# Third stage of a fused two-layer block: raw-weight loads 0 and 1 and context loads 2 and 3 issued from ScalarE instead of SyncE

## The chip, the cores and the metric

One NeuronCore of a Trainium2 chip runs the whole program. The metric is the device time of one execution in microseconds (us). Five engines work from their own instruction queues and meet through semaphores: TensorE (PE, matmuls), VectorE (DVE), ScalarE (ACT), GpSimd (POOL) and SyncE (SP), which only waits and issues DMAs. Both SP and ACT can issue DMAs; each has a DMA queue of its own (q1 is fed by SP, q10 by ACT in the profile), and the data are moved by the core's 16 DMA engines.

## The reference, cut to what matters

The program computes four residual blocks on x of 2048 tokens by 512 features (4 batches of 512). Each normalizes x first.

```python
x = x + _L0_xattn_ref(_layernorm(x), ctx_2048)                        # stage a: fp8-rounded product with the context
x = x + _L0_ffn_ref(_layernorm(x), gate_w, up_w, down_w, gate_s, up_s, down_s)   # stage b: SiLU-gated FFN, 1408 hidden
x = x + _L1_xattn_ref(_layernorm(x), ctx_2048, mask)                  # stage c: attention over the context
x = x + _L1_ffn_ref(_layernorm(x), w_gate, w_up, w_down)              # stage d: Hadamard-rotated ternary FFN, 2048 hidden

# _L1_xattn_ref
scores = einsum('bsd,bmd->bsm', hidden_states, memory_tokens) / sqrt(D)
scores = where(mask, scores, -1e30)
readout = einsum('bsm,bmd->bsd', softmax(scores), memory_tokens)

# weights of _L1_ffn_ref
scale = clip(mean(abs(w)), EPS)
wq = clip(round(w / scale), -1, 1) * scale
```

## The kernel before

The 2048 tokens are 16 tiles of 128 rows (NT = 16); four tiles share one context (TPB = 4), so contexts 0 to 3 serve tiles 0 to 3, 4 to 7, 8 to 11 and 12 to 15. Everything lives in SBUF in one hand-divided arena. Stages a and b are interleaved tile by tile and end at about 321 us; stage c, the "third stage", follows, and stage d takes the rest. No scheduler is involved: on each engine the order is that of the code, and every dependence is a semaphore that the code names.

Stage c, for tile k, in the order in which the tile passes through the engines:

- ACT normalizes the tile (`x_normal`, L775) and takes its fp16 high part (`x_high`, L782); POOL makes the low part (`x_low`, L494).
- SP turns both parts with two transposing DMAs, `c_x_turn` (L379 for the high part, L381 for the low one). Its buffer is one of two, so it waits until the scores of tile k-2 are done.
- PE makes the scores (`scores`, L1764, 16 matmuls of 128x512). DVE adds the mask and takes the row maximum (L1369, L1372), ACT takes the exponential (L817) and its fp16 high part (`p_high`, L788), POOL the low part (`p_low`, L499).
- SP turns both parts, `c_p_turn` (L387, L389), once the readout of tile k-2 is done.
- PE makes the readout (`readout`, L1782, 16 matmuls), and DVE adds it to X (L1354).

PE's order is scores(0), scores(1), scores(2), readout(0), scores(3), readout(1), scores(4), and so on: scores(k), readout(k-2).

Two more streams run beside this. The raw contexts (1 MB transposed and 1 MB plain each, `ctx2_load`, L370) are split into fp16 high and low parts: ACT makes the high parts (`context_high_parts`, L797), POOL the low parts (L505), except those of context 0, which DVE makes (L1439, semaphore `c_cv_first`). `conversions(k)` does part k mod 4 of context k/4+1 at tile k. The readout of tile 0 needs all four low parts of context 0. And the stage-d weights come in twelve raw chunks of 1 MB (`w1_load`), in two buffers: ACT takes the sign of w + threshold (`w1_sign`, L809), DVE rounds to ternary (`round_weights`, L1211). Chunk n is signed at tile n+1 and rounded at tile n+2; chunks 0 and 1 are loaded by SP (L394), chunks 2 to 11 by ACT (L801) right behind the sign of chunk n-1. The buffer of chunk 0 overlaps the down weights of stage b, that of chunk 1 the buffers of the earlier weight sums. Stage d begins with turns of tile 0 that wait for chunk 11 of 12 to be rounded.

In SP's order the weight loads stand between `c_x_turn(1)` and `c_x_turn(2)`, behind a wait for all residual sums of stage b (`b_add`, made by DVE at L1220); context load 2 stands between `c_x_turn(3)` and `c_p_turn(1)`, and context load 3 between `c_x_turn(7)` and `c_p_turn(5)`.

Of the kernel before, what the change touches and what calls it, by code (L numbers as in the profile page):

```python
# [7 lines left out]
P = 128  # L8
NT = T // P
TPB = NT // B  # L10
# [17 lines left out]
def fused_blocks(nc, x, ctx_t, ctx_n, mask, gate_t, up_t, down_t, gate_s, up_s, down_s,  # L28
# [7 lines left out]
    with ExitStack() as ctx:  # L36
# [79 lines left out]
        w1raw = [cut(24, 2048), cut(84, 2048)]  # L116
# [103 lines left out]
        def wait(eng, s, v):  # L220

            if not isinstance(v, int) or v > 0:
                eng.wait_ge(s, v)
# [32 lines left out]
        def at(k, n):  # L256

            return isinstance(k, int) and k == n
# [19 lines left out]
        def on(j):  # L278

            return not isinstance(j, int) or 0 <= j < NT  # L280
# [6 lines left out]
        def w1_chunk(n):  # L287

            if n < 8:
                return w1_src[n // 4][:, n % 4, :]  # L290
            return w1_src[2][:, 4 * (n - 8):4 * (n - 8) + 4, :]

        @block.sync
        def _(sp):
# [67 lines left out]
            sp.wait_ge(ds_ps, 1)  # L362
            sp.wait_ge(a_add, NT)
            def ctx2_load(e):
                if e == 2:
                    sp.wait_ge(c_cv_first, TPB)
                if e == 3:
                    sp.wait_ge(c_cv_lo, TPB)
                for t, src in enumerate((ctx_t, ctx_n)):
                    sp.dma_start(ctx_raw[e % 2][:, t, :, :], src[e].rearrange("(k p) m -> p k m", p=P)).then_inc(ctx2_in[e % 2], 16)  # L370

# [16 lines left out]
                sp.wait_ge(c_pl_r, j + 1)  # L388
                sp.dma_start_transpose(c_plT[u], c_pl[u]).then_inc(c_pq[u], 16)  # L389

            def w1_load(n):
                if n >= 2:
                    sp.wait_ge(w1_done, n - 1)
                sp.dma_start(w1raw[n % 2], w1_chunk(n)).then_inc(w1_in[n % 2], 16)  # L394

            c_x_turn(0)
            sp.wait_ge(w1a_done, 3 * NT)
            c_x_turn(1)
            sp.wait_ge(b_add, NT)
            w1_load(0)  # L400
            w1_load(1)
            for k in range(NT):
                if k < NT - 2:
                    c_x_turn(k + 2)
                if k in (1, 5):
                    ctx2_load(2 + k // 5)
                c_p_turn(k)

            def y_turn(j):
# [152 lines left out]
        def _(act):  # L562
# [227 lines left out]
            def context_high_parts(e, i):  # L790
# [5 lines left out]
                    wait(act, c_ro, TPB * (e - 1))  # L796
                nc.scalar.activation(ctx_p[e % 2][0][:, t, kk:kk + 2, :], ctx_raw[e % 2][:, t, kk:kk + 2, :], ACT.Copy).then_inc(c_cv_hi, 1)  # L797

            def w1_load(n):
                act.wait_ge(w1_done, n - 1)  # L800
                nc.scalar.dma_start(w1raw[n % 2], w1_chunk(n)).then_inc(w1_in[n % 2], 16)  # L801

            def w1_sign(n):
# [7 lines left out]

            def c_body(k, u):
                if on(k):
                    act.wait_ge(c_neg, 2 * k + 2)
                    wait(act, c_pl_r, k - 1)
                    wait(act, c_norm, 2 * k - 2)
                    nc.scalar.activation(c_p[u], bank(2 + u), ACT.Exp, bias=c_sm[:, u, 1:2], scale=SM_SCALE,  # L817
                                         accum_out=c_sm[:, u, 2:3]).then_inc(c_p_r, 1)
                    p_high(k)
                    if on(k + 3):  # L820
                        x_normal(k + 3)
                    if on(k + 3):
                        x_high(k + 3)
                    for e, i in conversions(k):
                        context_high_parts(e, i)
                    if 1 <= k < 13:
                        w1_sign(k - 1)
                    if 2 <= k < 12:
                        w1_load(k)
                if at(k, NT - 2):  # L830
                    d_high(0)
                if at(k, NT - 1):
                    d_round(0, 0)
                if at(k, NT):
                    d_turned(0, 0)
                    d_high(1)
# [1161 lines left out]
```

## Time and profile before

| what | value |
|---|---|
| time, median of 3 runs (lowest to highest) | 723.27 us (718.18 to 724.7) |
| the profiled execution: time, span in the profile | 720.0 us, 718.2 us |
| busy: PE, DVE, ACT, POOL | 91%, 82%, 66%, 51% of the span |
| LDWEIGHTS (PEld) busy | 52% |
| q1 (SP): packets, MB, share of the 16 engines | 167188, 71.94 MB, 43.4% |
| q10 (ACT): the same | 3408, 11.27 MB, 4.8% |
| chain that ended last, by engine | PE 48%, DVE 22%, ACT 10%, issue 7%, POOL 6%, DMA 5% |
| stage c in the span | about 321 to 445 us |

The page shows one execution. Busy shares are averages over the four stages; a wait is read from the timeline, where the number in brackets behind a row is the idle time of the engine just before it and what ended it. "SPq" and "ACTq" rows are DMA issues: their length is the time that the issuing queue was held, not the time of the transfer. The granted clock (PEclk) is 1.00 at 2.4 GHz and 0.50 at 1.2 GHz.

### The profile page before, as it was taken

What the parts mean: (1) busy time and instruction counts of PE and PEld (TensorE: products, weight loads), DVE (VectorE), ACT (ScalarE), POOL (GpSimd) and SP (SyncE); (2) the same over time, 40 slices, a digit from 0 to 9 for tenths busy, and PEclk for the clock granted to TensorE, in tenths of its full rate; (3) what the DMA queues carried; (4) which work ended last, traced back from release to release, by engine and by line L of the source; (5) the groups of instructions that cost most, each with busy time, mean ns of one, the idle gap of its engine ahead of it and who ended that gap; (6) DMA issues with size and microseconds to landing.
All of it is one profiled execution on the core that took longest, in us unless ns stands there. A gap on an engine that the chain in (4) does not pass through costs nothing.

```text
span 718.2 us, 12556 instructions
## 1 busy us (share of the span) xinstructions
PE 653.0 (91%) x4086; PEld 375.3 (52%) x4086; DVE 589.5 (82%) x1386; ACT 472.8 (66%) x965; POOL 368.5 (51%) x291
## 2 busy tenths in 40 slices
PE   1788899999999999997999999997999999999996
PEld 0365566656666676752444444444444445444543
DVE  6889899999998888365877764788999899999874
ACT  3747467766776556375878833567787887778734
POOL 2023032323232413165767631079999998999970
PEclk9999899999999999998999999999999999999999
DMA  8971233333341322718999930445556655655611
GB/s 215 249 257 23 82 85 92 101 93 102 76 110 23 110 68 69 246 31 249 242 304 250 240 78 18 88 74 88 104 108 128 118 102 115 134 117 116 109 56 45
DMA packets 173131, 88.22 MB, mean 123 GB/s; under 512 B 150546, under 2 KB 152594, under 8 KB 172052
## 3 DMA queue, kind: packets, MB, share of 16 engines
q1 hardware_dynamic: 167188, 71.94, 43.4%
q10 hardware_dynamic: 3408, 11.27, 4.8%
q0 software_dynamic: 2480, 4.33, 3.4%
q8 instruction: 28, 0.46, 0.3%
q14 instruction: 27, 0.22, 0.1%
HBM read 51.20 MB, written 4.19 MB: 77 GB/s over the span
## 4 chain that ended last, share of the span: by engine, by line
PE 48%; DVE 22%; ACT 10%; issue 7%; POOL 6%; DMA 5%; SPq 1%; POOLq 0%; ACTq 0%; DVEq 0%
PE ps L1840 10%; PE ps L1687 8%; PE ps L1764 7%; PE ps L1782 7%; PE ps L1702 5%; DMA arena<-arena 4%; PE ps L1820 3%; DVE X L1114 3%; PE ps L1912 2%; POOL arena L537 2%; POOL arena L538 2%; DVE arena L1204 2%; ACT arena L881 2%; DVE y_sm L1511 2%; PE ps L1880 2%
## 5 line engine op out<-in xcount | busy, mean ns | idle before, releaser
L1687 PE MATMUL ps<-arena 128*128 128x256 f16 x1408 | 162.7, 275 | 11.0 <-DVE arena L1204 5.7
L1687 PEld LDWEIGHTS ps<-arena 128*128 128x128 f16 x1408 | 137.0, 99 | 38.0 <-DVE arena L1204 9.1
L465 POOL TENSOR_TENSOR arena<-arena 128x256 f16<-128x256 f32 x88 | 57.7, 675 | 183.1 <-ACT arena L640 182.6
L1840 PE MATMUL ps<-arena 128*128 128x512 bf16 x512 | 118.3, 380 | 8.8 <-ACT arena L852 7.6
L537 POOL TENSOR_TENSOR arena<-arena 128x1024 f32<-128x1024 f32 x44 | 103.7, 2358 | 43.7 <-DVE arena L1485 40.2
L538 POOL TENSOR_TENSOR arena<-arena 128x1024 f32<-128x1024 f32 x44 | 104.0, 2364 | 0.0
L1840 PEld LDWEIGHTS ps<-arena 128*128 128x128 bf16 x512 | 47.7, 98 | 68.4 <-DVE arena L1477 10.2
L1702 PE MATMUL ps<-arena 128*128 128x512 f16 x352 | 78.6, 379 | 3.6 <-POOL arena L465 3.5
L633 ACT ACTIVATE arena<-ps,gs 128x256 f32<-128x256 f32 x88 | 40.7, 466 | 53.3 <-PE ps L1687 53.2
L1764 PE MATMUL ps<-arena 128*128 128x512 f16 x256 | 60.4, 391 | 5.5 <-DMA arena<-arena 5.5
L1912 PE MATMUL ps<-arena 128*128 128x512 bf16 x256 | 59.8, 379 | 1.5 <-ACT arena L925 1.5
L1782 PE MATMUL ps<-arena 128*128 128x512 f16 x256 | 57.7, 379 | 2.4 <-DMA arena<-arena 2.4
L1702 PEld LDWEIGHTS ps<-arena 128*128 128x128 f16 x352 | 33.7, 98 | 45.4 <-POOL arena L465 7.7
L1204 DVE SCALAR_TENSOR_TENSOR arena<-ps,us,arena 128x256 f32<-128x256 f32 x88 | 41.8, 479 | 18.0 <-ACT arena L633 17.7
L872 ACT ACTIVATE arena<-ps,f_sm 128x512 f32<-128x512 f32 x64 | 44.3, 692 | 15.7 <-PE ps L1840 14.9
L1466 DVE SCALAR_TENSOR_TENSOR ps<-ps,f_sm,arena 128x512 f32<-128x512 f32 x60 | 45.2, 754 | 10.9 <-ACT arena L872 10.9
L895 ACT ACTIVATE arena<-ps 128x512 f16<-128x512 f32 x60 | 35.6, 593 | 27.4 <-DVE ps L1466 27.4
L881 ACT ACTIVATE arena<-arena,y_sm 128x1024 f32<-128x1024 f32 x32 | 36.3, 1144 | 17.4 <-DVE y_sm L1525 17.4
L1477 DVE TENSOR_TENSOR arena<-ps,arena 128x512 f16<-128x512 f32 x60 | 41.2, 687 | 7.0 <-ACT arena L895 6.7
L1764 PEld LDWEIGHTS ps<-arena 128*128 128x128 f16 x256 | 25.5, 100 | 38.2 <-DMA arena<-arena 5.5
L1114 DVE SCALAR_TENSOR_TENSOR X<-ps,a_sm,X 128x512 f32<-128x512 f32 x56 | 41.9, 748 | 2.5 <-PE ps L1639 1.5
L1782 PEld LDWEIGHTS ps<-arena 128*128 128x128 f16 x256 | 24.9, 98 | 32.5 <-DMA arena<-arena 3.0
(160 smaller groups left out, 1208.7 us busy)
## 6 DMA issues: line engine op xcount, KB each, us to landing
arena<-in_ctx_t SPq DMA_DIRECT2D x7, 1024.0 KB, 6.1
arena<-in_wg_t SPq DMA_DIRECT2D x16, 256.0 KB, 3.9
arena<-in_wu_t SPq DMA_DIRECT2D x16, 256.0 KB, 4.4
arena<-in_wd_t SPq DMA_DIRECT2D x16, 256.0 KB, 5.0
arena<-in_ctx_n SPq DMA_DIRECT2D x4, 1024.0 KB, 9.7
arena<-in_wu_t ACTq DMA_DIRECT2D x4, 1024.0 KB, 5.7
arena<-in_wd_t ACTq DMA_DIRECT2D x4, 1024.0 KB, 5.8
out_x<-X SPq DMA_DIRECT2D x16, 256.0 KB, 2.5
```

The costliest lines, as they stand in the source:

```text
L465: nc.gpsimd.tensor_tensor(hl[:, c, at:at + 2 * P], b_h[n % 4], hh[:, c, at:at + 2 * P], ALU.subtract).then_inc(b_hl_r, 1)
L537: nc.gpsimd.tensor_tensor(b[:, :, 0, :], a[:, :, 0, :], a[:, :, 1, :], ALU.add).then_inc(d_bfp, 1)
L538: nc.gpsimd.tensor_tensor(b[:, :, 1, :], a[:, :, 0, :], a[:, :, 1, :], ALU.subtract).then_inc(d_bfp, 1)
L881: nc.scalar.activation(yr[:, 1024 * i:1024 * i + 1024], y_of(j)[:, 1024 * i:1024 * i + 1024], ACT.Copy, bias=ROUND_HALF, scale=y_sm[:, u, ...
L1114: V.scalar_tensor_tensor(tile_of(X, j), bank(2 + b), a_sm[:, u, 3, b:b + 1], tile_of(X, j), ALU.mult, ALU.add).then_inc(a_add if b == KD - ...
L1204: V.scalar_tensor_tensor(b_h[n % 4], bank(n % 2)[:, 2 * P:4 * P], us[:, c:c + 1], b_sil[n % 2], ALU.mult, ALU.mult).then_inc(b_h_r, 1)
L1687: last = M(bank(n % 2)[:, 2 * P * i:2 * P * i + 2 * P], W[:, b, c * P:c * P + P], part[:, b, at:at + 2 * P], start=(b == 0 and part is xhT ...
L1702: last = M(bank(6 + j % 2), part[:, c, at:at + P], dW[:, c, :], start=(c == 0 and part is hh), stop=(c == C0 - 1 and part is hl))
L1764: last = M(bank(2 + u), rows[u][:, b, :], part[:, 0, b, :], start=(b == 0 and rows is c_xhT and part is high), stop=(b == KD - 1 and rows ...
L1782: last = M(bank(6 + u), rows[u][:, b, :], part[:, 1, b, :], start=(b == 0 and rows is c_phT and part is high), stop=(b == KD - 1 and rows ...
L1840: last = M(bank(2 * (n % 2) + i), d_qT[u][:, b, :], W[:, b, D * n:D * n + D], start=(b == 0), stop=(b == KD - 1))
L1912: last = M(bank(down_bank(j)), yqT[u][:, c, :], Wd[:, c, :], start=(c == 0), stop=(c == C1 - 1))
```

## The change

Four DMA issues leave SP's queue and enter ACT's, in other places than they had:

- raw-weight chunk 0: at the head of tile 0 on ACT, before the exponential, waiting for the last down product of stage b (`b_dn`, by PE) instead of the last residual sum (`b_add`, by DVE);
- raw-weight chunk 1: behind the sign of chunk 0, at tile 1, as the later chunks are;
- context load 2: at the end of tile 2, behind the load of chunk 2;
- context load 3: at the end of tile 5, behind the load of chunk 5.

SP also loses the wait for `w1a_done` ahead of `c_x_turn(1)`, and is left in the third stage with the loads of contexts 0 and 1 and the transposing DMAs.

```diff
@@ SP
             def ctx2_load(e):
-                if e == 2:
-                    sp.wait_ge(c_cv_first, TPB)
-                if e == 3:
-                    sp.wait_ge(c_cv_lo, TPB)
                 for t, src in enumerate((ctx_t, ctx_n)):
...
-            def w1_load(n):
-                if n >= 2:
-                    sp.wait_ge(w1_done, n - 1)
-                sp.dma_start(w1raw[n % 2], w1_chunk(n)).then_inc(w1_in[n % 2], 16)
-
             c_x_turn(0)
-            sp.wait_ge(w1a_done, 3 * NT)
             c_x_turn(1)
-            sp.wait_ge(b_add, NT)
-            w1_load(0)
-            w1_load(1)
             for k in range(NT):
                 if k < NT - 2:
                     c_x_turn(k + 2)
-                if k in (1, 5):
-                    ctx2_load(2 + k // 5)
                 c_p_turn(k)
@@ ACT
+            def ctx2_load(e):
+                if e == 2:
+                    act.wait_ge(c_cv_first, TPB)
+                if e == 3:
+                    act.wait_ge(c_cv_lo, TPB)
+                for t, src in enumerate((ctx_t, ctx_n)):
+                    nc.scalar.dma_start(ctx_raw[e % 2][:, t, :, :], src[e].rearrange("(k p) m -> p k m", p=P)).then_inc(ctx2_in[e % 2], 16)
+
             def w1_load(n):
-                act.wait_ge(w1_done, n - 1)
+                if n == 0:
+                    act.wait_ge(b_dn, NT)
+                if n == 1:
+                    act.wait_ge(w1a_done, 3 * NT)
+                wait(act, w1_done, n - 1)
                 nc.scalar.dma_start(w1raw[n % 2], w1_chunk(n)).then_inc(w1_in[n % 2], 16)
@@ ACT c_body
                 if on(k):
+                    if k == 0:
+                        w1_load(0)
                     act.wait_ge(c_neg, 2 * k + 2)
...
                     if 1 <= k < 13:
                         w1_sign(k - 1)
-                    if 2 <= k < 12:
+                    if 1 <= k < 12:
                         w1_load(k)
+                    if k in (2, 5):
+                        ctx2_load(2 + k // 5)
```

SP's queue at the entry of stage c, before: the two transposes of tile 1's x, the weight loads, the transposes of tile 2's x, those of tile 0's probabilities, those of tile 3's x, context load 2, and the transposes of tile 1's probabilities.

```order
L379 DMA_TRANSPOSE arena<-arena 128x4x128 [waits c_x_high,w1a_done]
L381 DMA_TRANSPOSE arena<-arena 128x4x128 [waits c_x_low]
L394 DMA arena<-in_wg_t 128x2048 [waits b_added]
L394 DMA arena<-in_wg_t 128x2048
L379 DMA_TRANSPOSE arena<-arena 128x4x128 [waits c_x_high,c_scores]
L381 DMA_TRANSPOSE arena<-arena 128x4x128 [waits c_x_low]
L387 DMA_TRANSPOSE arena<-arena 128x4x128 [waits c_p_high]
L389 DMA_TRANSPOSE arena<-arena 128x4x128 [waits c_p_low]
L379 DMA_TRANSPOSE arena<-arena 128x4x128 [waits c_x_high,c_scores]
L381 DMA_TRANSPOSE arena<-arena 128x4x128 [waits c_x_low]
L370 DMA arena<-in_ctx_t 128x4x512 [waits c_ctx_first_low]
L370 DMA arena<-in_ctx_n 128x4x512
```

The same place of SP's queue now (lines are four lower).

```order
L375 DMA_TRANSPOSE arena<-arena 128x4x128 [waits c_x_high]
L377 DMA_TRANSPOSE arena<-arena 128x4x128 [waits c_x_low]
L375 DMA_TRANSPOSE arena<-arena 128x4x128 [waits c_x_high,c_scores]
L377 DMA_TRANSPOSE arena<-arena 128x4x128 [waits c_x_low]
L383 DMA_TRANSPOSE arena<-arena 128x4x128 [waits c_p_high]
L385 DMA_TRANSPOSE arena<-arena 128x4x128 [waits c_p_low]
L375 DMA_TRANSPOSE arena<-arena 128x4x128 [waits c_x_high,c_scores]
L377 DMA_TRANSPOSE arena<-arena 128x4x128 [waits c_x_low]
```

The transposes now follow one another, and no load stands between those of tile 1 and tile 2.

ACT's queue at the end of tile 2 and the start of tile 3, before: the conversion of context 1, the two signs of chunk 1, the load of chunk 2, and the exponential of tile 3.

```order
L797 ACTIVATE arena<-arena 128x1024 [waits ctx2_in1]
L809 ACTIVATE ps<-arena,thr 128x1024 [waits w1_first_half,prep,w1_in1]
L809 ACTIVATE ps<-arena,thr 128x1024 [waits w1_done]
L801 DMA arena<-in_wg_t 128x2048 [waits w1_done]
L817 ACTIVATE arena,c_sm<-ps,c_sm 128x512 [waits c_norm,c_p_low,c_neg_max]
```

The same place now.

```order
L782 ACTIVATE arena<-arena 128x1024 [waits ctx2_in1]
L806 ACTIVATE ps<-arena,thr 128x1024 [waits w1_first_half,prep,w1_in1]
L806 ACTIVATE ps<-arena,thr 128x1024 [waits w1_done]
L798 DMA arena<-in_wg_t 128x2048 [waits w1_done]
L790 DMA arena<-in_ctx_t 128x4x512 [waits c_ctx_first_low]
L790 DMA arena<-in_ctx_n 128x4x512
L816 ACTIVATE arena,c_sm<-ps,c_sm 128x512 [waits c_norm,c_p_low,c_neg_max]
```

The two context loads stand behind the load of chunk 2 in the same DMA queue, and ahead of the next exponential on the engine; at tile 5 it is the same with chunk 5 and context 3.

## Rows read from the trace of the kernel before

**Rows 1.** Chain that ended last, in order of time: start us, us, what
```profile
326.16 7.06 DMA arena<-arena
...
366.23 9.22 DMA arena<-arena
```

**Rows 2.** Timeline of PE, 320 to 411 us: start, length, engine, line, operation
```profile
321.18 7.07 PE L1764 MATMUL ps<-arena 128*128 128x512 f16 x32 [0.45 <-DMA arena<-arena]
333.26 6.29 PE L1764 MATMUL ps<-arena 128*128 128x512 f16 x16 [5.01 <-DMA arena<-arena]
339.39 3.62 PE L1782 MATMUL ps<-arena 128*128 128x512 f16 x16
342.84 3.62 PE L1764 MATMUL ps<-arena 128*128 128x512 f16 x16
...
375.49 3.63 PE L1782 MATMUL ps<-arena 128*128 128x512 f16 x16 [1.41 <-DMA arena<-arena]
```

**Rows 3.** Windows: stretch, its length, PE busy (x), granted clock, DMA share, GB/s
```profile
78.00:80.00 2.00, 0.00 (x0) 0.82 0.50 100
...
332.00:334.00 2.00, 0.74 (x2) 0.50 1.27 255
366.00:369.00 3.00, 3.00 (x16) 1.00 1.06 375
369.00:373.00 4.00, 4.00 (x20) 1.00 1.03 408
374.00:376.00 2.00, 0.59 (x4) 1.00 1.57 306
486.00:488.00 2.00, 0.24 (x6) 1.00 0.06 11
```

**Rows 4.** Timeline of SP's issues, 323 to 402 us
```profile
323.81 0.82 SPq L394 DMA_DIRECT2D arena<-in_wg_t  x2
324.83 1.28 SPq L379 DMA_TRANSPOSE arena<-arena  x1
326.16 1.86 SPq L381 DMA_TRANSPOSE arena<-arena  x1
...
364.98 1.20 SPq L387 DMA_TRANSPOSE arena<-arena  x1
366.23 4.87 SPq L389 DMA_TRANSPOSE arena<-arena  x1
...
401.10 1.27 SPq L389 DMA_TRANSPOSE arena<-arena  x1
```

**Rows 5.** Line L381's transposes, time from issue to landing
```profile
DMA to landing us min/median/max: 2.4/3.7/7.1
```

**Rows 6.** Timeline of all engines, 325 to 335 us (here DVE)
```profile
325.99 1.22 DVE L1439 TENSOR_TENSOR arena<-arena 128x1024 f16<-128x1024 f32 x1
...
330.67 3.01 DVE L1439 TENSOR_TENSOR arena<-arena 128x1024 f16<-128x1024 f32 x1
```

**Rows 7.** Timeline of ACT, 321 to 408 us
```profile
321.16 0.63 ACT L782 ACTIVATE arena<-arena 128x512 f16<-128x512 f32 x1
...
333.30 0.63 ACT L782 ACTIVATE arena<-arena 128x512 f16<-128x512 f32 x1 [1.55 <-DMA arena<-arena]
...
334.78 2.14 ACT L809 ACTIVATE ps<-arena,thr 128x1024 f32<-128x1024 f32 x2
...
404.31 0.69 ACT L817 ACTIVATE arena<-ps,c_sm 128x512 f32<-128x512 f32 x1 [1.11 <-DVE c_sm L1372]
...
407.96 1.10 ACT L809 ACTIVATE ps<-arena,thr 128x1024 f32<-128x1024 f32 x1
```

**Rows 8.** Line L801's weight loads of 1 MB, time from issue to landing
```profile
DMA to landing us min/median/max: 5.3/5.8/8.8
```

**Rows 9.** Line L370's context loads, SP's issues and their landing
```profile
L370 SPq DMA_DIRECT2D arena<-in_ctx_n x4: 507/930/1470, 289.0 to 363.7; - x4
...
DMA to landing us min/median/max: 5.6/8.5/12.9
```

## The prediction

> **What bounds the kernel now.** I read the page first: PE is busy for 91% of the span, so only a change that gives time back to PE counts. The chain that ended last comes next, over the third stage. Almost all of it is PE's own steps, but twice it passes through a transposing DMA: 7.06 us from the issue at 326.16 and 9.22 us from the issue at 366.23 [rows 1]. Then the timeline of PE around both. Scores(0) and scores(1) run back to back until 321.18 + 7.07 = 328.25; scores(2) starts at 333.26, behind 5.01 us of idleness that ended with a transpose; readout(5) starts at 375.49, behind 1.41 us of the same [rows 2]. Last the granted clock: scores(2) take 6.29 us, against a step of 342.84 - 339.39 = 3.45 us for the same 16 matmuls [rows 2], and the clock is 0.50 in that stretch, the lower of the two levels, 1.2 GHz [rows 3]. So the first stop costs 5.01 us of waiting and 6.29 - 3.45 = 2.84 us of slow matmuls, the second 1.41 us: 9.26 us in all, 1.3% of the time. The change can win little beyond that. Between the stops PE has no gap.
>
> Why the transposes are late is seen in SP's issues. The two weight loads (2 MB) go out at 323.81, the x transposes of tile 2 at 324.83 and 326.16 behind them in the same queue [rows 4]. The second lands about 7.1 us after its issue, where L381's fastest needs 2.4 and its median is 3.7 [rows 5]. The P transposes of tile 5 go out at 364.98 and 366.23, behind context load 3, and the latter holds SP's queue for 4.87 us [rows 4].
>
> **The weight loads, first stop.** What releases tile 2's x transposes is the end of scores(0), 321.18 + 3.62 = 324.8: their issue times, 324.83 and 326.16, stay. Their data no longer stand behind 2 MB. Chunk 1 goes out some 9 us later (below); chunk 0 goes out from ACT behind the x_high at 321.16 [rows 7], about 321.4, since PE's last down product is over by 321.18 - 0.45 = 320.7 [rows 2]; that is 2.4 us earlier than now. With the shortest landing of such a load, 5.3 us [rows 8], it is down at 326.7, with the median at 327.2, and the transpose issued at 326.16 meets hardly any of it. Its landing is then between 2.4 and 3.7 us [rows 5], 328.6 to 329.9. I take the fast end, because its cause of delay is what moves away: scores(2) start at 328.6, 0.35 us after PE is free, not at 333.26.
>
> Does the clock still fall? It fell in the idle stretch at 78 to 80 us, where PE was idle for 2 us and more, and in the stop of 5.01 us; it stayed at 1.00 through the stop of 1.41 us at 374 and one at 486 to 488, where PE was busy for only 0.24 of 2 us [rows 3]. Stops under 1.8 us leave it alone in this trace. So scores(2) take 3.45 us and end at about 332.1.
>
> Now another wait ends last. Readout(0) needs the low parts of context 0; the fourth is DVE's L1439 at 330.67, which takes 3.01 us, where the one at 325.99 takes 1.22 [rows 6]. It ends at 333.68. Nothing that the change moves lies ahead of it, so readout(0) starts at about 333.75, 1.65 us behind scores(2). Now it starts at 339.39 [rows 2]. **Term 1: 339.39 - 333.75 = 5.64 us gained.** (4.66 by the earlier start, 2.84 by the clock, less 1.65 of new wait, and 0.2 by which an end and a start overlap in the rows.) If L1439 took 1.22 us, the new wait would go and the term would be 7.3; if the transpose took 3.7 us, it would still be 5.64, hidden under L1439, as long as the clock stays.
>
> **Weight chunk 1.** It goes out behind the sign of chunk 0. That sign started at 334.78 after x_high(4), at 333.30, had waited 1.55 us for the late transpose [rows 7]. Without that wait the sign starts at 333.2 and the load goes out at about 333.4. It lands 5.8 us later, 339.2 [rows 8]. Its sign stands 407.96 - 404.31 = 3.65 us behind the exponential of its tile [rows 7]; exp(2) follows DVE, which is free at about 335 and needs 0.9, so the sign is due at 339.6. Just in time; a landing of 8.8 would hold ACT for 2.6 us.
>
> **What ACT's lateness costs.** Readouts follow one another every 2 x 3.45 = 6.9 us from 375.49, so one starts at 410.0 [rows 2]; its last P transpose goes out at 401.10 [rows 4]. With 2.7 us to land it could go out 6.2 us later. ACT also waits 1.11 us per tile for DVE [rows 7]. So 6 us of lateness on ACT reach no matmul, and 1.1 us per tile are made good. **Term 2: 0.**
>
> **The context loads, second stop.** On ACT they hold the queue for one issue of at most 1.47 us and one shorter [rows 9], twice: some 2 us, of which the second sign, already handed to the engine, covers half. Were one held as long as SP's transpose at 366.23 was, 4.87 us [rows 4], it would still be under 6. Hidden as above. In q10 they stand behind a 1 MB weight load and ahead of the next. Three MB take 3 / 0.375 = 8 us or 3 / 0.408 = 7.4 [rows 3], so the next chunk, issued a tile (6.9 us) later, lands 2 to 4 us after its sign is due, once per context. Hidden too.
>
> For the transposes the price is the same 3 MB in another queue. Between 366 and 373 us the two queues together move 375 and then 408 GB/s, the second figure with ACT's load beside SP's [rows 3]: they share one rate. A transpose issued as such a block began took 9.22 us [rows 1]. Its place allows 3 x 3.45 = 10.35 us from its release to its product, less the 1.25 between its two issues: 9.1. So a transpose caught at the worst moment is 0.1 us late, twice 0.1 for two loads. In the old kernel SP was also busy issuing the context, whose second half went out at 363.7, before it could issue the P transposes at 364.98 [rows 4, 9]; that goes. **Term 3: 1.41 - 0.2 = 1.2 us gained.**
>
> Here the Trainium skill speaks against the change. "DMA: Bandwidth & Descriptors", section "Issuing engines are not separate DMA queues", says that transfers from different engines run on the same 16 DMA engines and interleave, and that issuing from several saves only the issuing time. The 375 and 408 GB/s agree. Read strictly, it would leave the second stop in place; the rival for that is priced below from rows.
>
> **Sum.** 5.64 + 1.2 = 6.85 us. Nothing later in the kernel waits for anything but stage c: the first turn of stage d needs chunk 10 rounded at tile 14, and its sign is due at tile 11, three tiles (20.7 us) ahead. On the profiled execution: 720.0 - 6.85 = 713.15. That execution lies inside the runs shown (718.18, 723.27, 724.7); the four have a mean of 721.5, and I forecast 721.5 - 6.85 = 714.7 for a median of new runs.
>
> **Rivals.**
> A, the forecast: both stops gone, clock kept. Gain 5.6 to 8.5 (7.3 + 1.2); 713.0 to 715.9. Chance 0.60.
> B, the second stop stays and its like comes at the first context load, because small transposes take turns with large packets in the DMA engines. For it: the shared rate. Against it: 10.35 us of room against 9.22. Gain 5.64 - 1.41 = 4.2 at worst, 717.3. Chance 0.20.
> C, the clock still falls, because 0.35 and 1.65 us idle stand close together, or because chunk 0's load is slow (8.8 us: 330.2) and one gap is 2 us long. Gain 5.64 - 2.84 + 1.2 = 4.0 or less, 717.5; with a transpose that is as late as now, nothing is left of term 1 and the change does not do what it says (720.3). Chance 0.14.
> D, slower: the 3 MB blocks in q10 starve the transposes for longer than 9.22 us. If each of the two brings a stop like the first, 5.01 + 2.84 = 7.85 us, the sum is 15.7 - 6.85 = 8.9 us lost, 730.4. It decides from a landing of about 9.1 + 3.4 = 12.5 us at both places, where the two stops eat the 6.85; the longest context landing of 12.9 [rows 9] is for it, the transposes' 9.22 against it. Chance 0.06.
>
> **How the numbers follow.** The bound for a difference is 1% (7.2 us), about what a measurement of this kernel can tell. Case A lies on both sides of it: 6.85 is short by 0.4, but its range of 5.6 to 8.5 reaches further up than down, and the runs spread by 6.5 us; I put a little over half of A beyond it. So faster 0.34, same 0.60, slower 0.06. The range goes from 718.18 - 8.5 = 709.7 to the upper end of B and C, 720.3.
>
> **What would show it.** Right: scores(2) within 1.5 us of the end of scores(1), the clock 1.00 throughout stage c, readout(0) behind L1439's fourth part, no stop near tile 5, x transposes of tile 2 landing within 3.7 us. Wrong: ACT waiting over 6 us for chunk 3 or chunk 6, a stop at scores(5) or readout(3) behind context load 2, or a granted clock of 0.50 before 345 us.

## The result and the profile after

The changed kernel takes 727.46 us (median of 6 runs, 725.41 to 729.06), the kernel before 721.04 us beside it (6 runs, 718.07 to 724.7): 1.0094 times as long, 95% interval 1.0066 to 1.0122. That is 6.4 us slower by the medians and 6.8 by the ratio, where 6.85 us of gain were forecast, and it lies outside the range. Ratios here and below leave out executions in the chip's slower state (one of the ten of experiment 4, 732.83 us, and one of the kernel before, 729.3 us). The profiled execution took 725.41 us, its span is 723.6 us.

The timeline of PE in stage c, changed kernel (start, length, engine, line, operation; in brackets the idle time before it and what ended it). L1765 are the scores, L1783 the readouts:

```profile
320.00 3.61 PE L1765 MATMUL ps<-arena 128*128 128x512 f16 x16 [0.47 <-DMA arena<-arena]
326.47 8.38 PE L1765 MATMUL ps<-arena 128*128 128x512 f16 x32 [2.85 <-DMA arena<-arena]
334.68 3.62 PE L1783 MATMUL ps<-arena 128*128 128x512 f16 x16
...
349.09 3.63 PE L1783 MATMUL ps<-arena 128*128 128x512 f16 x16 [0.44 <-DMA arena<-arena]
356.66 5.18 PE L1765 MATMUL ps<-arena 128*128 128x512 f16 x16 [3.94 <-DMA arena<-arena]
...
382.92 5.30 PE L1765 MATMUL ps<-arena 128*128 128x512 f16 x16 [3.81 <-issue]
...
446.84 3.63 PE L1783 MATMUL ps<-arena 128*128 128x512 f16 x16 [0.98 <-DMA arena<-arena]
```

These answer to [rows 2]. The stop of 5.01 us ahead of scores(2) is gone. In its place stands one of 2.85 us ahead of scores(1), and two new ones stand behind the context loads: 3.94 us ahead of scores(5) and 3.81 us ahead of scores(8). The slow clock comes with three of them: 32 matmuls in 8.38 us instead of 7.07, 16 in 5.18 and in 5.30 instead of a step of 3.45. Together: 2.85 + 1.31 + 0.44 + 3.94 + 1.73 + 3.81 + 1.85 = 15.9 us, against 9.26 before. The stage shows the same from its ends: from the start of scores(0) to that of the last readout it took 119.99 us before (321.18 to 441.17) and takes 126.84 now (320.00 to 446.84), 6.85 more.

The chain that ended last (start, length, what) passes through the transposes here:

```profile
319.99 6.43 DMA arena<-arena
...
343.99 12.63 DMA arena<-arena
356.66 5.18 PE ps L1765 x16
...
379.11 3.81 issue
382.92 5.30 PE ps L1765 x16
```

They answer to [rows 1]: before, the chain had a transpose of 9.22 us behind a context load in the same queue; now it has another one, the low x part of tile 5, of 12.63 us beside one. "Issue" at 379.11 only says that the profile names no releaser. Other rows do (an issue of SP, the landing times of L377, and a row of ACT):

```profile
370.07 1.42 SPq L377 DMA_TRANSPOSE arena<-arena  x1
...
DMA to landing us min/median/max: 2.4/4.0/12.8
...
382.91 0.63 ACT L767 ACTIVATE arena<-arena 128x512 f16<-128x512 f32 x1 [4.09 <-DMA arena<-arena]
```

The low x part of tile 8 goes out at 370.07 and is L377's slowest, 12.8 us. It lands at 382.9, where both ACT (its next x_high) and PE (scores(8)) go on. So both long stops end with a low x transpose that took over 12.5 us. What went out around the first (L798 and L790 are ACT's loads of weights and contexts, L377 the low x transpose, L383 and L385 the P transposes):

```profile
319.97 0.33 ACTq L798 DMA_DIRECT2D arena<-in_wg_t  x1
319.99 1.19 SPq L377 DMA_TRANSPOSE arena<-arena  x1
...
340.95 0.33 ACTq L798 DMA_DIRECT2D arena<-in_wg_t  x1
341.32 0.61 ACTq L790 DMA_DIRECT2D arena<-in_ctx_t  x1
341.96 0.71 ACTq L790 DMA_DIRECT2D arena<-in_ctx_n  x1
343.99 1.59 SPq L377 DMA_TRANSPOSE arena<-arena  x1
345.68 3.22 SPq L383 DMA_TRANSPOSE arena<-arena  x1
346.70 0.35 ACTq L798 DMA_DIRECT2D arena<-in_wg_t  x1
348.94 4.12 SPq L385 DMA_TRANSPOSE arena<-arena  x1
```

Chunk 0 goes out 0.02 us before the low transpose of tile 1, and that one lands 6.43 us later. Around context 2, ACT sends chunk 2, the context and, 5.75 us after chunk 2, chunk 3: 4 MB in a row. From 344 to 358 us the DMA share of no window of 2 us is below 0.97 (at 342 to 344 it is 0.69); the windows (stretch, length, PE busy (x), granted clock, DMA share, GB/s), against [rows 3]:

```profile
324.00:326.00 2.00, 0.00 (x0) 0.93 1.13 214
326.00:328.00 2.00, 1.53 (x4) 0.50 0.83 113
...
350.00:352.00 2.00, 2.00 (x11) 1.00 1.08 361
352.00:354.00 2.00, 0.72 (x4) 1.00 1.13 428
354.00:356.00 2.00, 0.00 (x0) 1.00 0.99 350
356.00:358.00 2.00, 1.34 (x4) 0.61 1.33 255
```

**What the packets show.** The trace holds every packet with its queue, size and start. A transpose is 512 packets of 256 bytes (18 ns each, 32 per DMA engine). Weight chunks 0 to 7 move in packets of 8 KB (309 ns), chunks 8 to 11 and the contexts in packets of 2 KB (84 ns). Starts in the 0.5 us from each time on, changed kernel, all 16 engines:

```
from us   SP's queue (transposes, 256 B)   ACT's queue (loads)
344.0       0                               24 of 8 KB
347.5      85                               86 of 2 KB
349.0      82                               82 of 2 KB
350.5      80                               83 of 2 KB
353.5      27                               27 of 8 KB
354.5      28                               27 of 8 KB
355.5     459                                0
```

From 346 to 355.5 us the two queues take turns packet for packet: one turn carries 256 bytes of transpose against 2 or 8 KB of load. Beside 2 KB packets a transpose moves about 150 packets per us and needs 512 / 150 = 3.4 us, beside 8 KB packets about 50 per us and 10 us, alone 920 to 1100 per us and 0.5 us. As an estimate from these rates, a pair of transposes beside a long load is 7 to 20 us behind.

They do not always take turns. Where nothing else moves, a transpose's first packet starts 1.17 to 1.18 us after its issue (16 cases in the kernel before, the changed one and kernel 8 below). The low x part of tile 1 (issued at 319.99) and the low P part of tile 2 (issued at 341.24) would so have begun 0.2 and 0.3 us behind the first packets of chunks 0 and 2. While the 128 packets of each chunk started (320.96 to 324.46, 342.10 to 345.80), 14 packets of transposes did, all beside the chunk's last ones. So these two waited the chunk out although it was in the other queue. In kernel 8 below it is so for all six chunks whose packets lie between 343 and 382 us: between the first and the last quarter of their packets, 8 transpose packets started in all. Chunk 3 found transposes already in line, and there the counts are equal. What decides between the two is not shown.

The 12.63 us are made of both. The low x part of tile 5 stands third in line, behind the low P part of tile 2 (which lands after 7.8 us) and its own high part (9.7 us). The first of them waits for chunk 2 to pass, the three then take turns with the context and, at the end, with chunk 3.

### The profile page after: what moved, and what is told of

Read it like the earlier page. It is cut to its first block, busy times and chain, and to the rows that moved or that the text cites. A ratio compares the mean times of both kernels' runs of the same rounds, so it can differ in the third digit from the quotient of the medians.

```text
span 723.6 us, 12555 instructions
## 1 busy us (share of the span) xinstructions
PE 654.9 (91%) x4086; PEld 375.8 (52%) x4086; DVE 587.3 (81%) x1386; ACT 472.3 (65%) x965; POOL 367.2 (51%) x291
## 4 chain that ended last, share of the span: by engine, by line
PE 46%; DVE 21%; ACT 10%; issue 8%; POOL 7%; DMA 5%; SPq 2%; POOLq 0%; ACTq 0%; DVEq 0%
PE ps L1841 11%; PE ps L1688 7%; PE ps L1765 6%; PE ps L1783 6%; PE ps L1703 5%; DMA arena<-arena 4%; PE ps L1821 3%; PE ps L1913 3%; DVE X L1115 3%; POOL arena L522 2%; POOL arena L523 2%; DVE arena L1205 2%; ACT arena L882 2%; PE ps L1881 2%; DVE y_sm L1512 2%
## 5 line engine op out<-in xcount | busy, mean ns | idle before, releaser
L1765 PE MATMUL ps<-arena 128*128 128x512 f16 x256 | 62.3, 401 | 11.1 <-DMA arena<-arena 7.3
L1783 PE MATMUL ps<-arena 128*128 128x512 f16 x256 | 57.7, 379 | 1.4 <-DMA arena<-arena 1.4
L1467 DVE SCALAR_TENSOR_TENSOR ps<-ps,f_sm,arena 128x512 f32<-128x512 f32 x60 | 45.2, 754 | 11.8 <-ACT arena L873 11.8
L1765 PEld LDWEIGHTS ps<-arena 128*128 128x128 f16 x256 | 25.9, 102 | 45.7 <-issue 11.1
L1783 PEld LDWEIGHTS ps<-arena 128*128 128x128 f16 x256 | 24.8, 98 | 31.6 <-DMA arena<-arena 2.1
```

Of the source, the lines that this page charges most:

```text
L1765: last = M(bank(2 + u), rows[u][:, b, :], part[:, 0, b, :], start=(b == 0 and rows is c_xhT and part is high), stop=(b == KD - 1 and rows ...
L1783: last = M(bank(6 + u), rows[u][:, b, :], part[:, 1, b, :], start=(b == 0 and rows is c_phT and part is high), stop=(b == KD - 1 and rows ...
```

## Experiments

Each ratio is to the kernel before, run beside it on the same chip (medians of before 719.9 to 720.6 us); its interval, at 95%, is behind it. Code cuts are marked with dots. The first four take the change apart and try smaller turns and shorter blocks.

**1. The weight loads alone** (the changed kernel, context loads back in SP's queue).

```diff
+                if k in (1, 5):
+                    ctx2_load(2 + k // 5)      # SP, as before
                 c_p_turn(k)
...
@@ ACT
-                    if k in (2, 5):
-                        ctx2_load(2 + k // 5)
```

> The weight half of the change alone: chunks 0 and 1 go out from ACT, context loads 2 and 3 stay where they were in SP's queue. Theory T (turns): the 16 DMA engines serve the two queues in turns, packet by packet, so the small packets of a transpose in one queue crawl beside the large packets of a load in the other; what the change lost, it lost at the two context loads in ACT's queue. Then this kernel keeps the early gain (readout(0) about 4.7 us earlier than before, as in the changed kernel) and has no stop of 3.9 us at scores(5) and scores(8): 721.0 - 3.5, within 715 to 719. Rival S (slack): the late stops come because stage c runs earlier and has used up the room of the other engines, whoever issues the contexts: then a stop of 3 to 4 us appears near tile 5 here too, about 726. Rival L (ACT late): loads on ACT make its exponentials late; chunks 0 and 1 are only a sixth of that, so little change against before, 719 to 722.

Measured: 725.68 us (8 runs), 1.0062 (1.0023 to 1.0101). PE in stage c:

```profile
327.02 9.91 PE L1769 MATMUL ps<-arena 128*128 128x512 f16 x32 [3.11 <-DMA arena<-arena]
...
348.03 6.19 PE L1787 MATMUL ps<-arena 128*128 128x512 f16 x16 [4.20 <-DMA arena<-arena]
...
381.11 5.02 PE L1787 MATMUL ps<-arena 128*128 128x512 f16 x16 [2.72 <-DMA arena<-arena]
```

The weight loads alone make the kernel slower. The stop at scores(1) is there, and stops at both context loads too, although these stand where they stood. The time is that of rival S (about 726), and T's 715 to 719 missed. Two things changed for the contexts. PE reaches them sooner. And chunk 1, which ACT now issues at 336.79, runs beside context 2: its packets start from 340.73 to 344.02 with the context's between them, while no transpose packet starts. In the kernel before, ACT issued no load before 344.42. Readout(0) starts 336.76 - 320.30 = 16.46 us after scores(0).

**2. The context loads alone** (the kernel before, `ctx2_load` of contexts 2 and 3 on ACT at tiles 2 and 5).

> The context half alone: context loads 2 and 3 go out from ACT behind chunks 2 and 5, chunks 0 and 1 stay in SP's queue. T: the first stop stays as before (5.0 us and the lower clock), and two stops of 3 to 4 us with a clock fall each appear behind the context loads where before had one of 1.4: 721.0 + 10, within 727 to 733. S: stage c runs late here as it did before, the other engines have room, so no long stop: 720 to 722.

Measured: 726.65 us (5 runs), 1.0091 (1.0064 to 1.0118). The profiled execution (721.03 us, the shortest of the five) has the old first stop and two new ones, here of PE, and no slow clock behind these:

```profile
331.50 5.01 PE L1768 MATMUL ps<-arena 128*128 128x512 f16 x16 [4.81 <-DMA arena<-arena]
...
356.74 3.63 PE L1768 MATMUL ps<-arena 128*128 128x512 f16 x16 [2.97 <-DMA arena<-arena]
...
380.74 3.61 PE L1768 MATMUL ps<-arena 128*128 128x512 f16 x16 [3.11 <-issue]
```

A transpose of x took up to 12.1 us there, so the long landing comes with the context loads alone. This execution is 5.6 us below the median, so the stops shown are less than what the change costs in the median. Each half alone costs about as much as both together: 0.6% (0.2 to 1.0) and 0.9% against 0.9%. The costs don't add.

**3. Smaller turns** (the changed kernel, each chunk as four DMAs whose rows are 2 KB; the same bytes).

```diff
-                nc.scalar.dma_start(w1raw[n % 2], w1_chunk(n)).then_inc(w1_in[n % 2], 16)
+                for q in range(4):
+                    src = w1_chunk(n)[:, D * q:D * q + D] if n < 8 else w1_chunk(n)[:, q, :]
+                    nc.scalar.dma_start(w1raw[n % 2][:, D * q:D * q + D], src).then_inc(w1_in[n % 2], 16)
...
```

> The changed kernel with each weight chunk fetched by four DMAs of 256 KB with rows of 2 KB, where chunks 0 to 7 were one DMA with rows of 8 KB; all else is equal, and the moved bytes too. T: a transpose gets one packet per packet of the load; beside 2 KB packets it gets four times as many turns as beside 8 KB packets. The block behind a context load is two weight chunks and one context, and half of it now lets the transposes through: the landing of 12.6 us falls to 9 to 10, and each of the two long stops shrinks from 3.9 us to under 2: 720 to 724. If only bytes count (sharing by bytes, or plain waiting until the other queue is empty), landing and stops stay, 727 to 730; the three more issues per chunk hold ACT's queue 1 us longer.

Measured: 724.51 us (10 runs), 1.0057 (1.0040 to 1.0075). The low x transposes take at most 8.8 us instead of 12.8, and the stop at scores(1) falls from 2.85 to 1.57 us, as smaller turns would have it. The slowest of the other three kinds do not all get faster: high x 9.7 to 10.6 us, high P 11.3 to 9.3, low P 9.4 to 11.1. Stops of 1.79, 3.01 and 4.11 us stay, now ahead of readouts, where under 2 us were expected. As an estimate, 4 MB at 0.4 MB per us are 10 us in which the transposes run at a sixth of their speed alone.

**4. Shorter blocks** (the changed kernel, each context in halves of 1 MB, issued by ACT at tiles 2, 4, 6 and 8).

> The changed kernel with each late context in two halves of 1 MB, two tiles apart (context 2 at tiles 2 and 4, context 3 at tiles 6 and 8), since its second half is first read two tiles after its first. T: the block in ACT's queue is then at most 2 MB per tile (about 5.3 us of 6.9) and ends before the next chunk goes out, so the transposes get through in every tile; the stops of 3.9 us fall below 1 and the clock stays: 715 to 719. L or any theory of the number of loads on ACT: as many bytes and issues as in the changed kernel, so about 727.

Measured: 725.5 us (10 runs, 720.42 to 732.83), 1.0057 (1.0026 to 1.0088). The profiled execution, of 729.17 us, shows something new. PE, then the windows of DMA:

```profile
363.14 5.09 PE L1769 MATMUL ps<-arena 128*128 128x512 f16 x16 [8.66 <-DMA arena<-arena]
```

```profile
352.00:354.00 2.00, 2.00 (x11) 1.00 2.37 112
354.00:356.00 2.00, 0.49 (x3) 1.00 0.24 68
```

The expected 715 to 719 missed. For 4 us the engines move 112 and 68 GB/s instead of some 350, while the first packets of a chunk, 8 KB each, take up to 7636 ns instead of 309. A transpose lands 17.6 us after its issue. The same is seen in three other kernels (last section).

**5. Chunk 0 clear of tile 1** (the kernel before; chunk 0 by SP behind the turns of tile 1 as soon as the last down product is done, chunk 1 by ACT at tile 1).

```diff
-            sp.wait_ge(w1a_done, 3 * NT)
             c_x_turn(1)
-            sp.wait_ge(b_add, NT)
+            sp.wait_ge(b_dn, NT)
             w1_load(0)
-            w1_load(1)
...
@@ ACT
-                    if 2 <= k < 12:
+                    if 1 <= k < 12:
                         w1_load(k)
```

> The kernel before with chunk 0 in SP's queue between the x transposes of tiles 1 and 2 (waiting for the last down product), and chunk 1 from ACT at tile 1; contexts 2 and 3 on SP as before. Theory T+S (a transpose crawls beside a load in the other queue, and waits out a load ahead of it in its own; and the third stage has room for one such block per pair only when it runs late): the x transposes of tile 1 are clear of chunk 0, those of tile 2 stand behind 1 MB only, so scores(1) and scores(2) lose under 1 us and readout(0) starts within 1.7 us of scores(2)'s end, some 5.6 us earlier than before. Then the stops seen with the weight half alone come at the contexts, 4.2 us with a clock fall of 2.7 at readout(1) and 2.7 with 1.6 at readout(5), against 1.4 before: in all 721 - 5.6 + 9.8, about 725, within 720 to 727. If the first stop's removal is passed on whole (rival P, my prediction's view), 714 to 716.

Measured: 723.64 us (10 runs), 1.0038 (1.0010 to 1.0065). PE:

```profile
328.68 3.63 PE L1762 MATMUL ps<-arena 128*128 128x512 f16 x16 [1.57 <-DMA arena<-arena]
332.60 3.63 PE L1780 MATMUL ps<-arena 128*128 128x512 f16 x16 [0.29 <-DVE arena L1437]
...
350.68 5.43 PE L1780 MATMUL ps<-arena 128*128 128x512 f16 x16 [7.76 <-DMA arena<-arena]
```

Here the first stop goes as the prediction had it: the clock stays, and readout(0) waits for DVE's fourth low part. It starts 12.56 us after scores(0); before it was 339.39 - 321.18 = 18.21. And here the 5.65 us are lost again, by a stop of 3.06 us ahead of scores(3) and by 7.76 us and a slow readout behind the first context load. The profiled execution took 727.07 us, 3.4 more than the median, and has a standstill like kernel 4's (18 GB/s at 334 to 336 us) just ahead of the first, so it may show more loss than is usual.

**6. Halves in SP's queue** (kernel 5, each context in two halves behind the P turns of tiles 1, 3, 5 and 7).

```diff
-                if k in (1, 5):
-                    ctx2_load(2 + k // 5)
                 c_p_turn(k)
+                if k in (1, 3, 5, 7):
+                    ctx2_half(2 + k // 5, k // 2 % 2)
...
```

> As the kernel with chunk 0 on SP, and each late context in two loads of 1 MB on SP, each right behind the P transposes of a tile (1, 3, 5, 7) instead of 2 MB ahead of those of tiles 1 and 5. T+S: a block is now 1 MB of context beside 1 MB of weights, 5.3 us, inside the 10.35 us that a pair of transposes has; no stop over 1 us after scores(2), the clock stays: 713 to 717, faster than before by 0.6 to 1%. If stops come from the number of bytes per stage or from ACT, they stay, 722 to 726.

Measured: 722.78 us (10 runs, 720.16 to 728.25), 1.0055 (1.0025 to 1.0085). The profiled execution, 720.81 us, is one of the short ones: readout(0) 12.55 us after scores(0), the clock 1.00 in all of stage c, and five stops of 0.87, 1.29, 2.00, 2.42 and 1.61 us at the later tiles, 8.2 us in all. No stop is large, but the gain is spent, and the expected 713 to 717 missed.

**7 and 8. No late contexts** (the changed kernel and the kernel before, without the loads of contexts 2 and 3; tiles 8 to 15 use contexts 0 and 1 again, so the output is not that of the program, but the arithmetic is the same).

```diff
-                act.wait_ge(ctx2_in[e % 2], 32 * (e // 2) + 32)
+                act.wait_ge(ctx2_in[e % 2], 32)
...
-                    if k in (2, 5):
-                        ctx2_load(2 + k // 5)
```

> The changed kernel without the loads of contexts 2 and 3: tiles 8 to 15 use what the buffers hold, so the output differs; all arithmetic stays. It prices the context loads in ACT's queue. T: the two long stops (3.9 and 3.8 us, 1.7 and 1.9 us of slow clock) go, the first stop at scores(1) (2.9 us and 1.3 of slow clock) stays: 727.5 - 11.5, 714 to 718. If ACT's own lateness makes them, 724 and above.

> The kernel before without the loads of contexts 2 and 3 (tiles 8 to 15 use contexts 0 and 1 again, so the output differs). Theory T (in the kernel before the late contexts cost only their visible stop): the stop of 1.41 us goes, the other stays, 1.0 to 2.0 us less than the kernel before: 718.5 to 719.5. Rival U (the late contexts cost more than their stop): the same cut gives 713.2 beside the moved weight loads, whose first stop is worth 3.5 us there; then this kernel lies near 716.7. Either way the difference to 713.2 is what moving the weight loads alone is worth where no context load follows.

Measured: the changed kernel 713.24 us (2 runs), 0.9897 (0.9850 to 0.9944); the kernel before 715.93 us (6 runs), 0.9947 (0.9928 to 0.9966). PE of the first, then of the second:

```profile
326.79 7.08 PE L1763 MATMUL ps<-arena 128*128 128x512 f16 x32 [2.98 <-DMA arena<-arena]
...
340.08 3.63 PE L1763 MATMUL ps<-arena 128*128 128x512 f16 x16 [2.76 <-DMA arena<-arena]
```

```profile
320.25 7.07 PE L1762 MATMUL ps<-arena 128*128 128x512 f16 x32 [0.44 <-DMA arena<-arena]
332.62 5.07 PE L1762 MATMUL ps<-arena 128*128 128x512 f16 x16 [5.30 <-DMA arena<-arena]
```

Without late contexts, moving the weight loads gains 0.9947 - 0.9897 = 0.0050, 3.6 us. This is weak: kernel 7 has two runs, the two intervals overlap in 0.9928 to 0.9944, and the difference is uncertain by about 0.005 itself. In the two profiles, readout(0) starts 13.51 us after scores(0) in kernel 7 and 17.27 in kernel 8, 3.8 us sooner, but 2.76 us are lost again ahead of scores(3), and the whole stage is only 0.8 us shorter (116.75 against 117.51). What the late contexts cost is clearer: 1 - 0.9947, 3.8 us (2.4 to 5.2), in the kernel before, and 1.0094 - 0.9897 = 0.0197, 14.2 us (about 10 to 18), in the changed one. The change loses some 10 us at the contexts.

**9 to 11. Other ways to keep the gain.** Kernel 9 is kernel 6 with rows of 2 KB, kernel 10 the kernel before with rows of 2 KB, kernel 11 the kernel before with context halves behind the P turns.

> The kernel with chunk 0 on SP and the contexts in halves behind the P transposes, with every weight chunk fetched by four DMAs of rows of 2 KB. In the traces so far, the DMA engines came nearly to a standstill for 2 to 7 us five times, always in a chunk of 8 KB rows whose first packets fell into the middle of a transpose (two of them in e6_halves_behind_p, at 356 and 373 us); with rows of 2 KB none has been seen. Theory H (the standstill belongs to large packets meeting a transpose, and the crawl to their length): no packet over 2.5 us, no stop over 1.5 us behind the first readout: 713 to 718. Rival: such stops come from phases alone, whatever the packets: 721 to 725, like e6.

> The kernel before with the same four DMAs per chunk, nothing else changed: the price or gain of the packet size by itself. The first stop stays (2 MB ahead in the same queue, in 2 KB rows at about the same rate), so does the 1.4 us stop: 718 to 722. H expects no gain here, since the kernel before shows no standstill; three more issues a chunk hold ACT's and SP's queues 1 us longer each.

> The kernel before with the late contexts in halves behind the P transposes on SP, weights as before. T: the first stop stays (5.0 us and 2.8 of slow clock), the 1.4 us stop at readout(5) goes, since a block is now 1 MB of context beside 1 MB of weights: 719.2, within 717 to 721. If the new places bring a chunk's start into a transpose, a standstill of 2 us or more appears instead and the gain is gone.

Measured: 724.64 us, 1.0053 (1.0020 to 1.0086); 727.24 us, 1.0076 (1.0045 to 1.0107); 723.37 us, 1.0039 (1.0019 to 1.0059); 10 runs each. Kernel 9 was expected at 713 to 718 and kernel 11 at 717 to 721 unless a standstill came, as it did; kernel 10 was expected to change nothing (718 to 722). All three came out above. With 2 KB rows in the kernel before, the first stop grows from 5.01 to 7.01 us, and a stop of 3.62 us with a slow clock comes at 399 us. Kernel 11 has the standstill again in its profiled execution, its longest (729.87 us), in the windows and with a stop of PE at 400 us, 20 us later:

```profile
374.00:376.00 2.00, 2.00 (x11) 1.00 2.76 272
376.00:378.00 2.00, 1.00 (x5) 1.00 0.18 67
```

```profile
400.54 5.88 PE L1764 MATMUL ps<-arena 128*128 128x512 f16 x16 [5.79 <-DMA arena<-arena]
```

**12. The same queue, sooner** (the kernel before, `w1_load(0)` and `w1_load(1)` wait for `b_dn` instead of `b_add`, nothing else).

> The kernel before with one wait changed: the two weight loads stay in SP's queue behind the second x turn, but wait for the last down product of the stage before (some 2.5 us sooner) and no longer for the last addition. Everything behind them stays as in the kernel before, no weight load enters another queue. Theory Q (turns between queues were the trouble, not early work): the 2 MB are down by 328, tile 2's transposes land about 329.5, the stop of 5.01 us shrinks to 1 to 1.5 us, the clock stays, readout(0) starts behind DVE's fourth low part near 333.7, 12.5 us behind scores(0), and since chunk 1 comes no later than before nothing is given back: 715 to 717. Rival S (whatever PE gains at the first stop is given back at the context loads, because P and its low parts then come no sooner): 720 to 724, with stops of 4 to 8 us together between tiles 3 and 7.

Measured: 719.22 us (12 runs), 0.9989 (0.9976 to 1.0003). PE and SP:

```profile
322.81 7.07 PE L1764 MATMUL ps<-arena 128*128 128x512 f16 x32 [0.44 <-DMA arena<-arena]
334.30 6.49 PE L1764 MATMUL ps<-arena 128*128 128x512 f16 x16 [4.42 <-DMA arena<-arena]
340.62 3.62 PE L1782 MATMUL ps<-arena 128*128 128x512 f16 x16
```

```profile
322.80 1.19 SPq L381 DMA_TRANSPOSE arena<-arena  x1
324.04 1.06 SPq L394 DMA_DIRECT2D arena<-in_wg_t  x2
```

Neither theory's numbers held. The load goes out 1.23 us after scores(0) start instead of 2.63, since SP first has to issue tile 1's transposes; the stop shrinks from 5.01 to 4.42 us, and readout(0) comes 17.81 us after scores(0) instead of 18.21. The loads went out 1.4 us sooner and the stop shrank by 0.6 us, so most of what was won ahead of the queue did not reach PE. The clock falls as before. It is the only variant with all the work that isn't slower, and it isn't measurably faster.

## Why the prediction was wrong, point by point

**What bounds the kernel** was read rightly: PE, with two stops in stage c, both behind transposes. 9.26 us was the sum of the visible stops; kernel 8 shows that the late contexts alone cost 3.8 us (2.4 to 5.2) where the second stop shows 1.41. In its profile stage c is 2.5 us shorter (117.51 against 119.99): besides the 1.41, scores(2) run 1.2 us less at the slow clock (5.07 us against 6.29). Where the rest lies is not settled.

**Term 1, 5.64 us: the arithmetic held, the premise failed.** The working took chunk 0 to go out "about 321.4" and asked only whether it would meet the transpose issued at 326.16. It went out at 319.97, which, counted from the start of scores(0) (320.00 now, 321.18 before), is 321.15 in the older trace, so that time was right. But the low transpose of tile 1 goes out in the same moment, in the kernel before too (SP's issues there):

```profile
321.18 1.19 SPq L381 DMA_TRANSPOSE arena<-arena  x1
```

Beside chunk 0 it landed after 6.43 us: its packets started only when those of chunk 0 were through. PE stopped for 2.85 us one tile earlier than before, and 1.31 us went to the slow clock. From scores(0) to readout(0) it is 334.68 - 320.00 = 14.68 us, against 18.21: 3.5 us gained up to there. With chunk 0 out of the way (kernels 5 and 6) the distance is 12.56 and 12.55 us, where the prediction's own is 333.75 - 321.18 = 12.57: the release by scores(0), the new bound at DVE's fourth low part and the clock were all right. The step that failed is "meets hardly any of it": it holds for tile 2 and was never asked of tile 1. It made term 1 too large by 2.1 us.

**Term 2, 0: held, as far as ACT goes.** The context issues held ACT's queue for 0.61 and 0.71 us. What ACT's being free brought was the other half: it ran ahead and sent chunk 3 only 5.75 us behind chunk 2, so the block in its queue was 4 MB, not the 3 MB of the working.

**Term 3, +1.2 us: the step that lost the case.** "A transpose issued as such a block began took 9.22 us" priced a transpose behind a load in the same queue, which sent nothing until the load was through and then ran alone. In another queue the transposes first waited for the chunk ahead of the context and then took turns with the load, packet by packet, with three of them in line. The landings are 12.63 us for tile 5 and 12.8 for tile 8, where 9.1 fitted, and the stops cost 0.44 + 3.94 + 1.73 + 3.81 + 1.85 = 11.8 us, against 1.41: 10.4 lost instead of 1.2 gained. Kernels 7 and 8 bear it out: the late contexts cost some 10 us more in ACT's queue than in SP's.

**Rivals.** D, at a chance of 0.06, had the mechanism, both places and almost the size: it decides from a landing of 12.5 us at both places, and 12.63 and 12.8 were measured. It gave 8.9 us lost, and 6.8 were. B named the taking of turns and then priced it by the same 9.22 us. So the right mechanism stood in the prediction with the wrong price, and D with a chance set by that price. The sentence cited there, that queues of several engines interleave on the same 16 DMA engines (the Trainium skill, "DMA: Bandwidth & Descriptors", section "Issuing engines are not separate DMA queues"), agrees with the trace from 346 to 355.5 us, 82 packets against 82 per half microsecond, and not with the 3.5 us of chunk 0, where transposes got no turn until its last packets. It spoke against the change, and "interleave" should have been asked per packet, not per byte.

**"Passed on whole".** The sum let every microsecond won at scores(2) reach the end. Kernels 1, 5 and 6 reach readout(0) 1.8, 5.7 and 5.7 us sooner after scores(0) than before and give that back by 400 us. In all three the later stops are larger or more than before. Why is not separated: chunk 1 loaded beside context 2 (kernels 1 and 5), standstills (kernels 5 and 6), or work of POOL and DVE that comes no sooner when PE does. For the last speaks that kernel 6 has a stop of 1.29 and one of 1.61 us that ended with POOL's low parts of a context.

**The signs named ahead.** "A stop at scores(5) behind context load 2" and "a granted clock of 0.50 before 345 us" both came. ACT's wait for chunk 3 or 6 did not; its longest waits there, 4.88 and 4.09 us, ended with the two late transposes.

## What to carry to other kernels

When a load is moved out of the queue of small transfers on which PE waits, ask not only what it no longer stands in front of but what it now shares the DMA engines with. In these traces the small stream got at best one of its packets for each large one, and beside a chunk that it met with nothing in line before it, none until the chunk's last packets. Behind a load in its own queue a transpose waited once and then ran alone; beside one it was slow for as long as the other queue had work, and an engine that runs ahead makes that block longer than the load. Before crediting a gain early in a stage, look for the next place with a similar stop, and ask whether it has room for a PE that comes sooner.

## What the runs showed of the hardware

- Two queues that both had a backlog took turns packet for packet: 85 to 86, 82 to 82, 80 to 83 per 0.5 us with 2 KB packets, 27 to 27 and 28 to 27 with 8 KB (changed kernel).
- But a transpose issued as a chunk of 8 KB packets began or while it ran, with no other in line before it, got no turn until the chunk's last packets: 14 of its packets against 128 at 321 to 324.5 and at 342 to 346 us in the changed kernel, and the same at all six chunks from 343 to 382 us in kernel 8.
- In the kernel before, the context load in SP's own queue took turns with ACT's chunk, and the transposes behind it then ran alone.
- A near standstill: the 8 KB packets at the start of a chunk took 2.2 to 7.6 us instead of 0.31 in kernels 4, 5, 6 and 11 (up to 7636 ns at 352 us in kernel 4, 3351 at 333 in kernel 5, 5379 at 373 in kernel 6, 5380 at 375 in kernel 11), and the data rate fell to 18 to 149 GB/s in windows of 2 us. Each time the chunk's first packets fell into the middle of a transpose, but they did so at 335.7 us in the changed kernel too, and there took at most 1.34 us. No packet over 2 us is in the profiled executions of the kernel before, the changed one and kernels 1, 2, 7, 8 and 12. Kernels 3, 9 and 10, with 2 KB rows, show at most 2.8 us, none of them a load's packet. What causes it was not found.
- The clock: behind idle stretches of PE of 2.85 us (changed kernel) and 3.11 us (kernel 1) it was at 0.50, behind 2.97 and 3.11 us in kernel 2 and 2.98 us in kernel 7 it stayed at 1.00. The length of the stop alone does not decide.
- Issuing one transpose held SP's queue for 1.19 us where the DMA engines were free, for 4.26 us at most in stage c of the changed kernel, 4.87 in the kernel before, and 8.53 in kernel 4, at its standstill.
- Some variants spread wider from run to run than the kernel before beside them: kernel 5 from 719.58 to 728.85 us and kernel 6 from 720.16 to 728.25, the kernel before from 718.05 to 723.61; the changed kernel (725.41 to 729.06) and kernel 3 (722.09 to 726.48) do not. A chunk that meets a transpose in one execution and not in the next would do that; no two executions of one variant were profiled to show it.
